# First attention: the order of ScalarE's output copy and GpSimd's scaling within a turn

## The reference

```python
x = x + L0_attn(layernorm(x))   # 8 heads of 64, K and V from a latent of rank 64
x = x + L0_ffn(layernorm(x))    # 256 -> 1024 -> 1024 -> 1024 -> 256, silu, gelu, gelu
x = x + L1_attn(layernorm(x))   # 16 heads of 16, rotary
x = x + L1_ffn(layernorm(x))    # 256 -> 768 -> 256, silu
```

## Time and profile before

| | us |
|---|---|
| median of 3 runs | 2667.78 (2667.09 to 2669.75) |
| the profiled execution | 2667.85 |
| its span, first to last instruction | 2666.1 |
| mean granted clock of TensorE | 0.963 of full |
| busy: PE, DVE, ACT, POOL | 2457.5, 1514.9, 1358.1, 1000.4 |
| the first attention | from the start to about 945 |

### The profile page before, as it was taken

One profiled execution on the slowest core, in us unless ns is written; L12 is line 12 of the kernel. 1 busy time (PEld: TensorE's weight loads), 2 busy tenths in 40 slices (PEclk: granted clock), 3 DMA queues, 4 the chain that ended last, 5 costly groups with the idle time before them and its releaser, 6 DMA issues.

```text
span 2666.1 us, 38943 instructions
## 1 busy us (share of the span) xinstructions
PE 2457.5 (92%) x15333; PEld 1486.9 (56%) x15333; DVE 1514.9 (57%) x1965; ACT 1358.1 (51%) x1816; POOL 1000.4 (38%) x656
## 2 busy tenths in 40 slices
PE   6888888888888979999999999999999999999988
PEld 4434444444444458878878788544444444444677
DVE  6565665566656431432132222589889889797354
ACT  3344434434343434444344444367777777677533
POOL 1454464465464724654564565330000000000343
PEclk8989999999989989999999999999999999999999
DMA  2111211212111144555555555622322222311222
GB/s 71 40 42 56 70 64 51 70 52 69 39 50 48 31 152 160 179 173 183 171 176 182 180 184 170 177 75 51 71 50 39 63 45 43 70 42 26 63 74 76
DMA packets 139912, 241.81 MB, mean 91 GB/s; under 512 B 28272, under 2 KB 88688, under 8 KB 139376
## 3 DMA queue, kind: packets, MB, share of 16 engines
q1 hardware_dynamic: 139728, 239.29, 30.0%
HBM read 198.20 MB, written 52.03 MB: 94 GB/s over the span
## 4 chain that ended last, share of the span: by engine, by line
PE 53%; POOL 5%; DVE 2%; ACT 2%; issue 2%; DMA 0%; SPq 0%; POOLq 0%; DVEq 0%; ACTq 0%
PE m_R L110 38%; PE m_O L110 10%; PE m_X L110 3%; ACT m_P L1541 1%; POOL m_act1l L1799 1%; POOL m_t L1807 1%; POOL m_t L1809 1%; DVE m_ln_x L181 1%; PE m_X L1943 1%; POOL m_t L1811 1%; PE m_X L202 1%; POOL m_ln_rstd L176 1%; POOL m_comp L1816 0%; DVE m_ln_stat L159 0%; DVE m_mraw L1682 0%
## 5 line engine op out<-in xcount | busy, mean ns | idle before, releaser
L1682 DVE TENSOR_REDUCE m_mraw<-m_R 128x2 f32<-128x1024 f32 x512 | 625.7, 1224 | 88.4 <-PE m_R L110 84.0
L1541 ACT ACTIVATE m_P<-m_R 128x1024 f32<-128x1024 f32 x512 | 524.3, 1025 | 173.0 <-PE m_R L110 170.5
L538 ACT ACTIVATE a_P<-a_S 128x1024 f32<-128x1024 f32 x256 | 248.6, 1023 | 178.6 <-PE a_S L110 178.0
L110 PE MATMUL m_O<-m_P,m_V 128*17 128x256 f32 x4096 | 334.9, 399 | 2.8 <-ACT m_P L1541 1.1
L661 DVE TENSOR_REDUCE a_mraw<-a_X 128x2 f32<-128x1024 f32 x168 | 205.4, 1222 | 140.2 <-PE a_X L110 140.2
L110 PE MATMUL a_O<-a_P,a_V 128*64 128x512 f32 x1024 | 283.9, 681 | 0.0
L819 POOL TENSOR_TENSOR a_accp<-a_accp,a_P 128x1024 f32<-128x1024 f32 x96 | 229.9, 2395 | 90.0 <-ACT a_P L538 80.3
L110 PE MATMUL m_R<-m_Q,m_K 64*128 64x512 f32 x1024 | 259.8, 504 | 3.3 <-DVE m_mraw L1682 3.0
L1799 POOL TENSOR_TENSOR m_act0l<-m_xf,m_act0h 128x512 fp32r<-128x512 f32 x128 | 165.3, 1294 | 244.2 <-ACT m_xf L1605 135.4
L110 PE MATMUL m_R<-m_act0h,m_wt 128*128 128x512 f32 x640 | 251.4, 393 | 0.2 <-POOL m_act0l L1799 0.2
L110 PE MATMUL m_R<-m_act0l,m_wt 128*128 128x512 f32 x640 | 250.8, 392 | 0.0
(11 more groups left out here) (235 smaller groups left out, 4301.3 us busy)
## 6 DMA issues: line engine op xcount, KB each, us to landing
m_wt<-wcopy SPq DMA_DIRECT2D x176, 512.0 KB, 3.3
m_ln_x<-x SPq DMA_DIRECT2D x24, 512.0 KB, 4.0
m_xres<-x SPq DMA_DIRECT2D x96, 128.0 KB, 3.2
m_K<-bounce_k SPq DMA_DIRECT2D x96, 128.0 KB, 4.2
m_Q<-bounce_q SPq DMA_DIRECT2D x192, 64.0 KB, 2.6
a_tile<-in_L_ffn_tiles SPq DMA_DIRECT2D x22, 512.0 KB, 3.8
wcopy<-in_L_ffn_tiles SPq DMA_DIRECT2D x22, 512.0 KB, 4.8
x<-m_xres SPq DMA_DIRECT2D x64, 128.0 KB, 1.7
```

The source lines that it names most:

```text
L110: return pe.eng.matmul(out, lhsT, rhs, start=start, stop=stop, skip_group_check=True)
L538: act.eng.activation(P[n % NP][:, :, :], psS[n % 2][:, :, :], ACT.Exp, scale=SCALE).then_inc(s_exp)
L1541: act.eng.activation(P[h % 4][:, :, :], pair(key)[:, :, :], ACT.Exp, scale=SCALE).then_inc(R.free(key))
L1682: dve.eng.tensor_reduce(mraw[u % 2][:, at, :], pair(key)[:, :, :], AX.X, ALU.max).then_inc(R.free(key))
```

## The change

Two calls are moved, one on ACT and one on POOL; no instruction is added or removed. In turn (u, 0) ACT makes the copy of the output of unit u - 1 as the last thing of the turn, behind the query's rounding, the latents, the norm's scalings and the tile's rounding. POOL makes the scaling of unit u - 2's output in front of the turn's additions, not behind them.

```diff
@@ scalar, in the loop over turns
                 for n in (2 * m, 2 * m + 1):
                     exponent(n)
-                if j == 0 and u:
-                    keep_out(u - 1)
                 if query_at(u, j):
                     query_high(query_at(u, j))
                 if latent_at(u, j):
...
                 if tile_at(u, j) and tile_at(u, j)[1] == "round":
                     tile_high(tile_at(u, j)[0])
+                if j == 0 and u:
+                    keep_out(u - 1)
             keep_out(NU - 1)
@@ gpsimd, in the loop over turns
                 if out_at(u, j):
                     out_low(*out_at(u, j))
+                if j == 0 and u >= 2:
+                    scale_out(u - 2)
                 if m:
                     for n in (2 * m - 2, 2 * m - 1):
                         add(n)
-                if j == 0 and u >= 2:
-                    scale_out(u - 2)
```

## The result

The changed kernel takes 2536.04 us (median of 4 runs, 2530.83 to 2540.80) against 2667.44: a ratio of 0.9507, 95% interval 0.9488 to 0.9526, 131 us less. The forecast was 2556 with a low end of 2536, so the time lies at the fast end (by the ratio, 0.9507 x 2667.44 = 2535.9, just beyond it): the direction and the chain held, and some 20 us of gain were not in the sum.

A forecast was written before the change was run, and what follows sets the result against it. PE, 92% busy, was held in the first attention by a chain of ACT's late query rounding and DVE's row maxima, and by its lowered clock. Waits 65.6 + clock 46 = 111.6 us; 2667.85 - 111.6 = 2556 us, range 2536 to 2606.

The forecast's parts named there:

- ACT's rounding 2.33 us earlier, 0.81 us of PE's wait left: Query's rounding in (u, 0) no longer waits behind the output's copy; PE's 3.14 us stall in (u, 1) loses 2.33.
- The copy behind everything costs nothing: ACT's output copy (line 546) starts as before in a common unit; 0 to 5 us, taken as 0.
- The clock: In the first attention PE's clock stays up in nearly all units; 46 us gain, bounds 0 and 53.
- My sign that the clock would stay up: Trace before: clock stayed full after the 2.06 us wait at 845.50 and never fell from 834 to 908 us.
- The side effect on line 683: DVE's addition for t = 5 gets about 1 us shorter as POOL waits for inverses; 0 to 3 us, taken as 0.
- another term: The clock term: (u, 0) waits of 1.5 to 1.9 us from the first batch's output weights stay, leaving four lower stretches.
- Rival 2: POOL's delayed addition collides with DVE's line 687, 29 us of gain lost: 2585 us, up to 2620; chance 0.07.
- Rival 1: The clock still falls once in each unit, so only the idle goes: 2602 us; chance 0.09.
- inverses hold PE: Rival 3: POOL's scaling at (u, 0) waits for inverses, delaying addition, merge and PE's sums: 2715 us; chance 0.04.
- a new owner: Rival 4: PE finds another bank taken, under a quarter of the gain comes: about 2640 us; chance 0.05.
- shorter waits of PE: PE's stalls before the second maxima product of (u, 1), plus the K remainder's waits in three latent units: 65.6 us.
- the term that stood at nothing: POOL's scaling ahead of the turn's additions, hidden by POOL's 9.43 us idle before the merge: taken as 0.

The follow-up runs named there:

- two extra reductions: The changed kernel plus two unused 1.2 us reductions on DVE behind the query remainder, to bring PE's wait in (u, 1) back: 2630.26 us, ratio 0.9865.
- The kernel with the late remainder: Against the changed kernel, DVE makes its addition for t = 7 in front of the query remainder instead of behind it: 2596.23 us, ratio 0.9721.
- the tile check one turn later: Against the changed kernel, the weight tiles' check starts one turn later, moving DVE's comparison (line 707) from (u, 0) to (u, 1): 2547.99 us, ratio 0.9556.

## Why the prediction was right, and where it failed

- *ACT's rounding 2.33 us earlier, 0.81 us of PE's wait left*: right. 0.74 us in this unit, 0.74 to 0.84 in most; DVE's idle 0.98 against 1.04. Turn (u, 1) took 10.33 us before, 6.27 after: 4.06 less, forecast 4.04.
- *The copy behind everything costs nothing*: right. PE's weighted sums waited 0.5 us for line 546 in the whole stage.
- *The clock*: right in mechanism, low in size. I took 46 us. The time at the lower clock went from 105.8 us to 3.4, worth 51.2. The kernel with two extra reductions prices one fall at 1.7 us by itself. My sign that the clock would stay up was weaker than I wrote: of the three waits of 2.0 to 2.1 us in the trace of before, the one at 761.05 was met by the lower clock.
- *The side effect on line 683*: **this is the step that failed.** I saw that the addition would lose its second microsecond, and wrote "PE waits only half a microsecond there, in a few units: 0 to 3 us of gain, taken as 0". The runs show 15.5 us for it in the medians, behind ACT's move (the change against ACT's move alone), and 24 us for POOL's move by itself, of which 13 are shorter waits. The numbers stood in the earlier trace rows: 53 waits of 101.4 us for row maxima. The 26 that I had listed in (u, 1) make 21 x 3.15 + 8.7 + 0.45, and the three latent units some 4.5 more, together 80 us; 24 waits of 21 us were left over, and they are those in (u, 0). I did not subtract. The four of them that come from the output weights, 6.7 us, stayed, as I had said of them in another term; most of the other 15 went. The matmul rows also show that wait too short: in a unit of before, PE's product at 324.78 has 0.49 us of idle, but its weights' load 0.92, and turn (u, 0) lost 0.76 (6.72 us against 5.96).
- *Rival 2, the collision with line 687*: rightly rejected as a rule, but by 0.17 us and not by the 1.6 that I gave, which is luck: the scaling started 3.9 us behind the first issue of the inverses, not 3.4, and (u, 0) itself became 0.8 us shorter. In four of the 32 units the additions did meet, and line 687 took 1.6 to 2.4 us. The kernel with the late remainder shows what lies on the other side: 60 us when lines 687 and 707 both lose.
- *Rival 1* (clock), *3* (inverses hold PE) and *4* (a new owner) fell: the clock stayed up, and from 74 us on none of PE's waits is for POOL, and none reaches 2 us.

Sum by parts, over the whole attention:

| | forecast | measured |
|---|---|---|
| shorter waits of PE | 65.6 | 113.3 - 32.9 = 80.4 |
| clock | 46 | (105.8 - 3.4) / 2 = 51.2 |
| together | 111.6 | 131.6, of the 132.8 by which the stage became shorter |

The stage gained 21.2 us more than the sum. By its length, 14.1 of them are the place of POOL's scaling (the stage is so much longer with ACT's move alone), the term that stood at nothing. The other 7.1 came with ACT's move, 5.2 of them by the clock. The 4.2 us that the profiled execution gained behind the stage are chance: nothing is changed there, and 77 us of it were at the lower clock before and 63 after.

## What to carry to other kernels

An output copy that waits for the end of a turn belongs behind whatever has its data earlier on the same engine; look for an idle stretch in front of a copy that the next engine's idle stretch mirrors. When a move changes the time at which GpSimd works, list every VectorE operation with two SBUF inputs that it will now meet or miss, on both sides, and give each race its margin. Judge a new order by the long waits that it leaves or makes, not by the typical unit alone: with the tile check one turn later the unit was 1 us shorter and the kernel 12 us slower. And when waits are taken from a list by hand, subtract their sum from the total of the waits view: what remains is somebody else's and has to be placed.

## What the runs showed of the hardware

- VectorE's two-input addition and GpSimd's take turns: 1.22 us alone, 3.06 when GpSimd started 0.4 us ahead, 3.44 when both started together; VectorE's comparison the same, 1.22 and 3.08 to 3.10. GpSimd's merge took 2.38 us when it started first and 3.22 when VectorE had started 0.2 us ahead.
- Waits of PE of 3.1 to 3.3 us were met by the lower clock in 21 of 21 cases in the kernel before, those of 3.0 to 3.2 us in 17 of 21 with two extra reductions, those of 1.9 to 2.0 us in 3 of 21 with one. But with the tile check one turn later waits of 1.57 us were met by it too (at 353 and 520 us). A fall cost 1.7 us.
- The runs of the changed kernel spread over 10 us (2530.83 to 2540.80) with mean clocks of 0.984 to 0.978; the slower had the lower clock. Behind the attention, its two traces have 63 and 56 us at the lower clock, in part in different places; what decides it is left open.
